# Where the projection of q and the state sums stand in TensorE's order, in a retention layer with a mixture of experts

## The chip, the cores and the metric

The kernel runs on one core of a Trainium2 chip. The metric is the device time of one execution in microseconds (us); lower is better. In the tables and rows PE is the tensor engine (PEld its weight loads), DVE the vector engine, ACT the scalar engine, POOL GpSimd and SP the engine whose queue issues most of the DMAs.

## The reference

Everything is float32. The input x has 4 batches of 1024 tokens with 256 channels. The first half is a retention layer with 16 heads of 16 channels, the second an expert layer; both have a residual.

```python
def attn(x):                       # on the layer norm of x
    q, k, v = x @ W_q.T, x @ W_k.T, x @ W_v.T      # split into 16 heads of 16
    decay = where(i >= j, gamma[head] ** (i - j), 0)
    a = einsum('bihd,bjhd->bhij', q, k) * decay / sqrt(16)
    y = einsum('bhij,bjhd->bihd', a, v)
    yn = (y - y.mean over tokens and head channels) / sqrt(var + 1e-5)
    return (yn * gn_weight + gn_bias) @ W_o.T
x = x + attn(layernorm(x))
x = x + ffn(layernorm(x))          # shared gated layer + two of 8 experts per token
```

The decay lets the product be computed in chunks: inside a chunk through scores, and across chunks through a state (the decayed sum of k times v of all earlier tokens) that is carried forward.

## The kernel before

**Phases.** The first half of the time is the retention phase, 16 steps h = 0 to 15, each over 256 tokens (a "part"): batch b = h // 4 and place in the batch s = h % 4. Behind it comes the expert phase, a loop over batches, which the diff doesn't touch. In the profiled execution step h = 0 begins at about 20.5 us and step 15 ends at about 225 us.

**Arithmetic.** A float32 product is made of three matmuls with operands that are split in a high and a low part (`split_product`, L289 to L296). A projection of 256 tokens is therefore 12 matmuls of 256 columns, all with line L294 in the profile.

**One step on TensorE** (`step`, L430). TensorE works on two parts at once, the scores and state of part h and the projections of part h + 1. The order before is: `project_k(h+1)` into `c_bank`, `state_sums(h)` (64 small matmuls, L378, into `a_bank`), in steps with s = 0 and b > 0 `head_means` (L408), `project_q(h+1)` into `b_bank`, `from_state(h)` (64 small matmuls of q with the state, L393, 48 of them where s = 0), `k_by_tokens(h+1)` (4 transposes, L343), then what is left of the previous batch (in s = 0 `head_vars` L412, in s = 1 `output_bias` L418, in s = 2 and 3 two `output` products each, 24 matmuls L294), `from_scores(h)` (L402), `project_v(h+1)`, `transpose_x(h+2)` (L304) and `scores(h+1)` (L364).

**One step on VectorE** (`step`, L870), strictly in this order: `mask_scores(h)` (4 operations, L782), `add_state(h)` (it waits for `state_sums(h)`; L792 or L795, then L798, which gives `s_ready`, and where s < 3 two small L803 that carry the state), `decay_k(h+1)` (L771, gives `kT_ready`), `decay_q(h+1)` (L776, gives `qT_ready`), in s = 0 `gn_spread` (four tiny operations, the last gives what `head_vars` waits for), the layer norm of part h + 3 (L748 to L761, with one tiny power on POOL in the middle), in s = 2 and 3 two residual sums (L861), `low_y(h)` (L812), `y_sums(h)` (L817), `low_x(h+2)` (L766), in s = 1 with b > 0 `low_wo` (L853).

**Waits that matter here.**

```python
# from_state(h), first lines                     # add_state(h)
pe.wait_ge(s_ready, h + 1)                       dve.wait_ge(s_done, h + 1)
# k_by_tokens(h), first line                     # project_k(h), first line
pe.wait_ge(kT_ready, h + 1)                      pe.wait_ge(xlo_ready, h + 1)   # low_x
```

`project_q` waits for nothing of its own in a step (L333); its bank `b_bank` was read out by `low_x`, for which `project_k` has waited. ScalarE copies between these: `spread_k` (L606) after `kT_ready`, `copy_k`, `high_y`, `high_x`, `copy_v`, and up to step 10 one piece of the expert weights (L638), which POOL then turns into its low part (L1068, `low_ffn`). In the steps h = 1 POOL also makes sums of the expert biases (L1107).

The order of every queue is written out by hand; only semaphores tie the engines to each other.

Of the kernel before, what the change touches and what calls it, by code (L numbers as in the profile page):

```python
# [17 lines left out]
PARTS = NBATCH * NSUP  # L18
# [35 lines left out]
def moe_retention(nc, xa, xs, wattn, gnw, gnb, sw1, sw3, sw2, w1, w2, sb1, sb3, b1, sb2, b2, decay, masks, out):  # L54
# [3 lines left out]
    with ExitStack() as ctx:  # L58
# [229 lines left out]
        def _(pe):  # L288
# [19 lines left out]
            def project_v(h):  # L308
                if h == 0:
                    pe.wait_ge(wlo_ready, 3)  # L310
                else:
                    pe.wait_ge(s_ready, h)
                for t in range(TILES):
                    w = [(xhi[:, c, t * P:(t + 1) * P], xlo[:, c, t * P:(t + 1) * P]) for c in range(CB)]
                    mm = split_product(a_bank[:, t * D:(t + 1) * D], w, [(wqkv_split.hi[:, 2, c, :], wqkv_split.lo[:, 2, c, :]) for c in range(CB)])
                mm.then_inc(v_done, 1)

            def project_channels(bank, i, done):
                x = [(xhi[:, c, :], xlo[:, c, :]) for c in range(CB)]
                for g in range(GROUPS):  # L320
                    w = [(wqkv_split.hi[:, i, c, g * P:(g + 1) * P], wqkv_split.lo[:, i, c, g * P:(g + 1) * P]) for c in range(CB)]
                    mm = split_product(bank[:, g * SUPER:(g + 1) * SUPER], w, x)
                mm.then_inc(done, 1)

            def project_k(h):
                pe.wait_ge(xlo_ready, h + 1)
                if h == 0:
                    pe.wait_ge(wlo_ready, 1)
                else:
                    pe.wait_ge(kexp_copied, h)  # L330
                project_channels(c_bank, 1, k_done)

            def project_q(h):  # L333
                if h == 0:
                    pe.wait_ge(wlo_ready, 2)
                project_channels(b_bank, 0, q_done)

            def k_by_tokens(h):
                pe.wait_ge(kT_ready, h + 1)
                for t in range(TILES):  # L340
                    for g in range(GROUPS):
                        o = (t * GROUPS + g) * P
                        mm = nc.tensor.transpose(c_bank[:, o:o + P], kT[:, g, t * P:(t + 1) * P], ident)  # L343
                mm.then_inc(kt_done, 1)
# [23 lines left out]
            def state_sums(h):  # L368

                pe.wait_ge(kexp_copied, h + 1)  # L370
                pe.wait_ge(v_copied, h + 1)
                for c in range(CPS):
                    n = 2 - c % 2
                    for g in range(GROUPS):
                        o = (g * CPS + c) * 32
                        for p in range(PAIRS):
                            r = g * PAIRS + p
                            mm = nc.tensor.matmul(a_bank[32 * p:32 * p + 32, o:o + n * 32].rearrange("p (n e) -> p n e", n=n),  # L378
                                                  kexp[:, c, r, :], vexp[h % 2][:, c, r, :].unsqueeze(1).broadcast_to([P, n, 32]),
                                                  start=(c == 0 and g == 0), stop=True, skip_group_check=True)  # L380
                mm.then_inc(s_done, 1)

            def from_state(h):
                pe.wait_ge(s_ready, h + 1)
                if h:
                    pe.wait_ge(y_stats, h)
                first = 0 if h % NSUP else 1
                for c in range(first, CPS):
                    for g in range(GROUPS):
                        o = g * SUPER + c * CH  # L390
                        for p in range(PAIRS):
                            at = slice(32 * p, 32 * p + 32)
                            nc.tensor.matmul(y_bank[at, o:o + CH], state[h % 2][at, g, c, :], qT[h % 2][at, g, c * CH:(c + 1) * CH],  # L393
                                             start=(c == first and g == 0), stop=False, skip_group_check=True)

            def from_scores(h):
                pe.wait_ge(pm_ready, (h + 1) * PAIRS)
                for c in range(CPS):
                    for g in range(GROUPS):
                        o = g * SUPER + c * CH  # L400
                        for p in range(PAIRS):
                            mm = nc.tensor.matmul(y_bank[32 * p:32 * p + 32, o:o + CH], vexp[h % 2][:, c, g * PAIRS + p, :],  # L402
                                                  pm[p][:, c * GROUPS + g, :], start=False, stop=True, skip_group_check=True)
                mm.then_inc(y_done, 1)

            def head_means(b, bank):
                pe.wait_ge(gn_aggr, b + 1)
                nc.tensor.matmul(bank[:, 0:GROUPS], headmean, y_mv[:, :, 0], start=True, stop=True).then_inc(gn_mean, 1)  # L408

            def head_vars(b, bank):  # L410
                pe.wait_ge(gn_e, b + 1)
                nc.tensor.matmul(bank[:, 8:8 + GROUPS], headmean, y_e[:], start=True, stop=True).then_inc(gn_var, 1)  # L412

            def output_bias(b, bank):

                pe.wait_ge(bb_ready, b + 1)
                for c in range(CB):
                    mm = nc.tensor.matmul(bank[:, 0:D], y_bb[:, c, :], wo_raw[:, c, :], start=(c == 0), stop=(c == CB - 1))  # L418
                mm.then_inc(ob_done, 1)

            def output(b, j, bank):
                if j == 0:
                    pe.wait_ge(ylo_ready, (b + 1) * NSUP)
                    pe.wait_ge(wolo_ready, b + 1)
                for i in range(2):
                    w = [(yhi[b % 2][:, c, 2 * j + i, :], ylo[b % 2][:, c, 2 * j + i, :]) for c in range(CB)]
                    mm = split_product(bank[:, i * D:(i + 1) * D], w, [(wo_hi[:, c, :], wo_lo[:, c, :]) for c in range(CB)])
                mm.then_inc(o_done, 1)

            def step(h):  # L430
                b, s = h // NSUP, h % NSUP
                if h + 1 < PARTS:
                    project_k(h + 1)
                state_sums(h)
                if b and s == 0:
                    pe.wait_ge(pm_ready, h * PAIRS + 1)
                    head_means(b - 1, p_bank[0])
                if h + 1 < PARTS:
                    project_q(h + 1)
                from_state(h)  # L440
                if h + 1 < PARTS:
                    k_by_tokens(h + 1)
                else:
                    transpose_x2(0, 0)
                    transpose_x2(0, 1)
                if b and s == 0:
                    head_vars(b - 1, p_bank[0])
                if b and s == 1:
                    pe.wait_ge(pm_ready, h * PAIRS + 2)
                    output_bias(b - 1, p_bank[1])  # L450
                if b and s >= 2:
                    for j in range(2 * (s - 2), 2 * (s - 2) + 2):
                        pe.wait_ge(pm_ready, h * PAIRS + (j + 1))
                        output(b - 1, j, p_bank[j])
                if h + 1 == PARTS:
                    transpose_x2(0, 2)
                    transpose_x2(0, 3)
                from_scores(h)
                if h + 1 < PARTS:
                    project_v(h + 1)  # L460
                    if h + 2 < PARTS:
                        transpose_x(h + 2)
                    scores(h + 1)

            def transpose_x2(b, j):

                half, c = j // CB, j % CB
                if j == 0 and not (isinstance(b, int) and b == 0):
                    pe.wait_ge(gelu_ready, b * NE)
                if c == 0:  # L470
                    pe.wait_ge(xn2_ready, b * 2 + (half + 1))
                for t in range(4):
                    mm = nc.tensor.transpose(t2_bank[j][:, t * P:(t + 1) * P],  # L473
                                             xl[:, 4 * half + t, c * P:(c + 1) * P], ident)
                mm.then_inc(t2_done, 1)
# [78 lines left out]
            for h in range(PARTS):  # L554
                step(h)
# [633 lines left out]
```

## Time and profile before

| | us |
|---|---|
| median of 3 runs | 468.68 |
| lowest and highest run | 466.65, 469.02 |
| the profiled execution, its own time | 470.15 |
| its span, first to last instruction | 468.3 |
| PE busy (matmuls) | 447.9 |
| DVE busy | 294.4 |
| ACT busy | 217.1 |
| POOL busy | 101.4 |
| mean granted TensorE clock, share of full | 0.982 |

The profiled execution took 470.15 us, of which 468.3 us are its span; the rest lies around it. Busy time of matmuls counts overlapping pieces once and has modelled ends, so the starts of matmuls are the better clock: the start of one group to the start of the next is what a group costs.

### The profile page before, as it was taken

Reading aid. Unit: us, or ns where it says so; the run is one execution under the profiler, and the core shown is the slowest. Engines: PE = TensorE matmul, PEld = TensorE weight load, DVE = VectorE, ACT = ScalarE, POOL = GpSimd, SP = SyncE. Lnnn points to the kernel's source line nnn. Section 1 sums busy time; section 2 is a strip of 40 time slices with the busy share of each in tenths; the row PEclk is TensorE's granted clock in tenths of the full one; section 3 lists DMA queues with packets and bytes.
Section 4 is the critical chain, followed back from the end, with each engine's and each line's share of the span. In section 5 each row is a group of like instructions: output and inputs, shape, how many; then the busy total and the mean of one; then the engine's idle time right before and its main releaser. Section 6 shows DMA issues by size and latency. Waiting matters only on the chain.

```text
span 468.3 us, 14948 instructions
## 1 busy us (share of the span) xinstructions
PE 447.9 (96%) x6574; PEld 411.6 (88%) x6574; DVE 294.4 (63%) x655; ACT 217.1 (46%) x416; POOL 101.4 (22%) x79
## 2 busy tenths in 40 slices
PE   6899998999898999978999999999999999999997
PEld 4899997989888999968798999889998899988996
DVE  6578986877789778685574644566445564455321
ACT  3455555544665535441525534355343552445521
POOL 2017522712326201410180110301103011030000
PEclk9999998999999999996999999999999999999999
DMA  7511242201531040200514010500105001030011
GB/s 255 196 56 72 70 149 82 70 25 49 168 153 71 3 161 26 92 3 1 203 69 179 1 46 1 225 0 0 45 0 224 0 0 45 2 132 0 1 46 45
DMA packets 9271, 34.75 MB, mean 74 GB/s; under 512 B 1665, under 2 KB 1921, under 8 KB 7041
## 3 DMA queue, kind: packets, MB, share of 16 engines
q1 hardware_dynamic: 8784, 33.15, 19.5%
q8 instruction: 45, 0.74, 0.7%
q10 hardware_dynamic: 432, 0.79, 0.6%
q14 instruction: 10, 0.07, 0.0%
HBM read 25.54 MB, written 8.39 MB: 72 GB/s over the span
## 4 chain that ended last, share of the span: by engine, by line
PE 84%; DVE 10%; issue 2%; ACT 1%; DMA 1%; POOL 0%; SPq 0%; DVEq 0%; ACTq 0%
PE bank L294 65%; PE bank L364 5%; PE bank L402 3%; DVE pm L782 3%; PE bank L393 3%; PE bank L378 2%; PE bank L473 2%; PE bank L343 2%; DVE wo_lo L853 1%; DMA xin<-xa 1%; PE bank L304 1%; DVE state L803 1%; PE bank L418 1%; ACT xhi L583 1%; DVE ln_st L917 1%
## 5 line engine op out<-in xcount | busy, mean ns | idle before, releaser
L688 ACT ACTIVATE xres<-bank,r1b 128x256 f32<-128x256 f32 x64 | 26.8, 469 | 55.5 <-PE bank L294 55.5
L673 ACT ACTIVATE sil<-bank,s1b 128x512 f32<-128x512 f32 x32 | 22.1, 689 | 63.0 <-PE bank L294 63.0
L294 PE MATMUL bank<-x2hi,sw_hi 128*128 128x512 f32 x128 | 51.0, 398 | 0.0
L294 PE MATMUL bank<-x2hi,sw_lo 128*128 128x512 f32 x128 | 50.9, 398 | 0.0
L294 PE MATMUL bank<-x2lo,sw_hi 128*128 128x512 f32 x128 | 50.3, 393 | 0.0
L949 DVE SCALAR_TENSOR_TENSOR gf<-bank,s3b,sil 128x512 f32<-128x512 f32 x32 | 23.9, 748 | 39.4 <-PE bank L294 39.4
L606 ACT ACTIVATE keo<-kT,msk 128x512 f32<-128x512 f32 x32 | 21.4, 715 | 56.2 <-DVE kT L771 56.2
L782 DVE TENSOR_TENSOR pm<-bank,msk 128x512 f32<-128x512 f32 x64 | 39.7, 681 | 6.2 <-PE bank L364 6.2
L294 PE MATMUL bank<-xhi,wqkv_hi 128*128 128x256 f32 x128 | 39.8, 311 | 2.3 <-DVE xlo L766 2.3
L967 DVE TENSOR_TENSOR xr<-bank,xr 128x256 f32<-128x256 f32 x32 | 13.6, 424 | 41.8 <-PE bank L294 41.8
L294 PE MATMUL bank<-xhi,wqkv_lo 128*128 128x256 f32 x128 | 36.4, 284 | 0.0
L294 PE MATMUL bank<-xlo,wqkv_hi 128*128 128x256 f32 x128 | 36.3, 284 | 0.0
L961 DVE TENSOR_TENSOR elo<-xres,ehi 128x512 fp32r<-128x512 f32 x32 | 22.1, 691 | 22.5 <-ACT ehi L692 22.5
L294 PE MATMUL bank<-x2lo,w_hi 128*128 128x256 f32 x128 | 36.2, 283 | 0.0
L294 PE MATMUL bank<-x2hi,w_lo 128*128 128x256 f32 x128 | 36.2, 283 | 0.0
L294 PE MATMUL bank<-x2hi,w_hi 128*128 128x256 f32 x128 | 36.2, 283 | 0.0
L1094 POOL TENSOR_TENSOR xr<-xr,slot_bias 128x2048 f32<-128x2048 f32 x4 | 18.5, 4626 | 81.7 <-DMA xr<-x_scratch 81.7
L294 PE MATMUL bank<-sw_hi,ghi 128*128 128x256 f32 x128 | 36.1, 282 | 0.0
L364 PE MATMUL bank<-qT,keo 32*128 32x64 f32 x1024 | 33.9, 282 | 2.3 <-DVE xres L861 2.3
L364 PEld LDWEIGHTS bank<-qT,keo 32*128 32x128 f32 x1024 | 31.7, 195 | 5.0 <-issue 5.0
L294 PE MATMUL bank<-w_hi,elo 128*128 128x256 f32 x128 | 36.0, 282 | 0.0
L294 PE MATMUL bank<-w_lo,ehi 128*128 128x256 f32 x128 | 36.0, 281 | 0.0
(119 smaller groups left out, 1277.8 us busy)
## 6 DMA issues: line engine op xcount, KB each, us to landing
xin<-xa SPq DMA_DIRECT2D x16, 256.0 KB, 3.8
w_raw<-w SPq DMA_DIRECT2D x8, 512.0 KB, 4.7
xres<-xs SPq DMA_DIRECT2D x4, 1024.0 KB, 5.0
x_scratch<-xres SPq DMA_DIRECT2D x4, 1024.0 KB, 4.9
xl<-x_scratch SPq DMA_DIRECT2D x4, 1024.0 KB, 5.6
xr<-x_scratch SPq DMA_DIRECT2D x4, 1024.0 KB, 4.8
out<-xr SPq DMA_DIRECT2D x8, 512.0 KB, 2.6
sw_raw<-sw SPq DMA_DIRECT2D x3, 512.0 KB, 4.9
```

Of the source, the lines that this page charges most:

```text
L294: mm = nc.tensor.matmul(o, w[c][l], x[c][r], start=first and c == 0 and j == 0, stop=last and c == n - 1 and j == 2)
L364: mm = nc.tensor.matmul(p_bank[p][:, o:o + CH], keo[at, c, g, :, :], qT[h % 2][at, g, c * CH:(c + 1) * CH], start=True, stop=True)
L393: nc.tensor.matmul(y_bank[at, o:o + CH], state[h % 2][at, g, c, :], qT[h % 2][at, g, c * CH:(c + 1) * CH], start=(c == first and g == 0), ...
L402: mm = nc.tensor.matmul(y_bank[32 * p:32 * p + 32, o:o + CH], vexp[h % 2][:, c, g * PAIRS + p, :], pm[p][:, c * GROUPS + g, :], start=Fals ...
L606: cp = nc.scalar.activation(keo[:, :, :, odd, :], kT[:].rearrange("p g (c j) -> p c g j", c=CPS), ACT.Copy, scale=parity[:, odd:odd + 1])
L673: nc.scalar.activation(sil[i % 2][:], h1_bank[i % 2][:], ACT.Silu, bias=s1b[:, m:m + 1]).then_inc(sil_ready, 1)
L688: ge = nc.scalar.activation(hf[q % 2][:, m, :], e_bank[q % 4][:, m * 2 * P:(m + 1) * 2 * P], ACT.Gelu, bias=r1b[:, e, m:m + 1])
L782: nc.vector.tensor_tensor(pm[p][:], p_bank[p][:].rearrange("p (a i) -> p a i", i=CH), causal.unsqueeze(1).broadcast_to([P, CPS * GROUPS, C ...
L949: nc.vector.scalar_tensor_tensor(gf[i % 3][:], h3_bank[i % 2][:], s3b[:, m:m + 1], sil[i % 2][:], ALU.add, ALU.mult).then_inc(gf_ready, 1)
L961: nc.vector.tensor_tensor(elo[k][:], hf[q % 2][:], ehi[k][:].bitcast(F32), ALU.subtract).then_inc(elo_ready, 1)
L967: nc.vector.tensor_tensor(xr[:, s, :], o_bank[s % 2][:, 0:D], xr[:, s, :], ALU.add).then_inc(o_ready, 1)
L1094: nc.gpsimd.tensor_tensor(xr[:], xr[:], slot_bias[:], ALU.add).then_inc(biased, 1)
```

## The change

`project_q(h+1)` is moved up in TensorE's order, from behind `state_sums(h)` (and `head_means`) to directly behind `project_k(h+1)`. `state_sums(h)` is then directly ahead of `from_state(h)`, but for `head_means` where there is one. It concerns the 15 steps with h + 1 < 16. No instruction is added or removed, and no other queue is touched.

```diff
                 if h + 1 < PARTS:
                     project_k(h + 1)
+                    project_q(h + 1)
                 state_sums(h)
                 if b and s == 0:
                     pe.wait_ge(pm_ready, h * PAIRS + 1)
                     head_means(b - 1, p_bank[0])
-                if h + 1 < PARTS:
-                    project_q(h + 1)
                 from_state(h)
                 if h + 1 < PARTS:
                     k_by_tokens(h + 1)
```

## Rows read from the trace of the kernel before

**Rows 1.** The page: busy time by engine, and the chain that ended last.

```profile
PE 447.9 (96%) x6574; PEld 411.6 (88%) x6574; DVE 294.4 (63%) x655; ACT 217.1 (46%) x416; POOL 101.4 (22%) x79
...
PE 84%; DVE 10%; issue 2%; ACT 1%; DMA 1%; POOL 0%; SPq 0%; DVEq 0%; ACTq 0%
```

**Rows 2.** Waits: engine, operation <- releaser; total us, times, longest us.

```profile
PE bank L393 <- DVE state L798: 4.5, 4, 1.7
```

**Rows 3.** Timeline, PE, step h = 2: start us, us, engine, line, operation.

```profile
43.17 0.39 PE L294 MATMUL bank<-xhi,wqkv_hi 128*128 128x256 f32 x1
...
44.58 0.28 PE L294 MATMUL bank<-xlo,wqkv_hi 128*128 128x256 f32 x1
44.79 0.91 PE L378 MATMUL bank<-vexp,kexp 128*32 128x64 f32 x64
45.62 0.39 PE L294 MATMUL bank<-xhi,wqkv_hi 128*128 128x256 f32 x1
...
47.25 1.10 PE L393 MATMUL bank<-qT,state 32*32 32x64 f32 x64
```

**Rows 4.** Timeline, PE: 24 large matmuls in a row, first start, next group's start.

```profile
97.18 0.36 PE L294 MATMUL bank<-wo_hi,yhi 128*128 128x256 f32 x1
...
100.23 0.49 PE L402 MATMUL bank<-pm,vexp 128*32 128x64 f32 x20
```

**Rows 5.** Timeline, DVE, step h = 2.

```profile
45.77 0.29 DVE L795 TENSOR_TENSOR state<-bank,state 128x128 f32<-128x128 f32 x1
...
46.42 0.39 DVE L803 TENSOR_SCALAR state<-state,msk 128x32 f32<-128x32 f32 x2
46.74 0.68 DVE L771 TENSOR_TENSOR kT<-bank,dec 128x512 f32<-128x512 f32 x1
...
52.69 0.69 DVE L766 TENSOR_TENSOR xlo<-bank,xhi 128x512 fp32r<-128x512 f32 x1
```

**Rows 6.** Timeline, step h = 9: the end of the state sums and what follows.

```profile
134.12 0.55 PE L378 MATMUL bank<-vexp,kexp 128*32 128x64 f32 x30 [0.44 <-issue]
...
134.73 0.29 DVE L795 TENSOR_TENSOR state<-bank,state 128x128 f32<-128x128 f32 x1 [0.69 <-PE bank L378]
```

**Rows 7.** Timeline, step h = 14: its start, the state's sum, the product that waits.

```profile
195.10 0.39 PE L294 MATMUL bank<-xhi,wqkv_hi 128*128 128x256 f32 x1
...
199.19 0.28 DVE L795 TENSOR_TENSOR state<-bank,state 128x128 f32<-128x128 f32 x1
...
199.85 0.36 PE L393 MATMUL bank<-qT,state 32*32 32x64 f32 x11 [0.60 <-DVE state L798]
```

**Rows 8.** Timeline, step h = 4 (s = 0): start, kT, head_vars, a gap.

```profile
64.62 0.39 PE L294 MATMUL bank<-xhi,wqkv_hi 128*128 128x256 f32 x1
...
68.72 0.68 DVE L771 TENSOR_TENSOR kT<-bank,dec 128x512 f32<-128x512 f32 x1
...
70.59 0.38 PE L412 MATMUL bank<-y_e,msk 128*128 128x2 f32 x2 [0.20 <-DVE y_e L833]
...
72.97 1.07 PE L402 MATMUL bank<-pm,vexp 128*32 128x64 f32 x28 [1.32 <-issue]
```

**Rows 9.** Timeline, PE, step h = 12 (s = 0): start and head_vars.

```profile
172.41 0.39 PE L294 MATMUL bank<-xhi,wqkv_hi 128*128 128x256 f32 x1
...
178.09 0.38 PE L412 MATMUL bank<-y_e,msk 128*128 128x2 f32 x2
```

**Rows 10.** Timeline, step h = 8: POOL's low part and DVE's carry.

```profile
121.45 2.39 POOL L1068 TENSOR_TENSOR w_lo<-w_raw,w_hi 128x1024 fp32r<-128x1024 f32 x1 [9.24 <-ACT w_hi L638]
...
122.15 1.86 DVE L803 TENSOR_SCALAR state<-state,msk 128x32 f32<-128x32 f32 x2
```

**Rows 11.** Timeline, POOL, step h = 2.

```profile
47.41 2.38 POOL L1068 TENSOR_TENSOR sw_lo<-sw_raw,sw_hi 128x1024 fp32r<-128x1024 f32 x1
```

**Rows 12.** Windows: stretch, length, busy time (instructions) of PE, PEld, DVE, ACT, POOL, PEclk, DMA share, GB/s.

```profile
64.60:78.90 14.30, 12.78 (x292) 11.61 (x288) 10.08 (x30) 6.44 (x14) 3.75 (x3) 0.88 0.41 132
...
143.80:158.80 15.00, 13.75 (x333) 12.76 (x326) 12.02 (x25) 7.64 (x15) 5.31 (x4) 1.00 0.13 48
...
209.30:220.00 10.70, 8.94 (x203) 8.54 (x204) 5.47 (x13) 0.79 (x3) 0.00 (x0) 0.52 0.02 4
```

## The prediction

> **What bounds the kernel now.** I read the page first. TensorE is busy for 96% of the span and is 84% of the chain that ended last, VectorE 10% [rows 1]. So a wait of TensorE in the retention phase is paid in full, unless TensorE is waiting there anyway. The list of waits says how often it stands at the product that is moved against the state sums: `from_state` waited for the state only 4 times, 4.5 us in all [rows 2], although there are 16 such products. The timeline of a plain step shows why. In step 2 `project_k` starts at 43.17, the state sums at 44.79, `project_q` at 45.62 and `from_state` at 47.25, without a gap [rows 3]. VectorE adds the state at 45.77, just behind the sums' modelled end of 44.79 + 0.91 = 45.70, and is through with it before 46.42 [rows 3, 5]. The 1.63 us of `project_q` cover this round trip through VectorE. The change takes the cover away.
>
> **The change in a plain step.** I count from the start of `project_k`.
>
> Before: `project_k` 1.62, sums 0.83, `project_q` 1.63, so `from_state` starts at +4.08 [rows 3].
>
> After, the two projections are one run of 24 large matmuls. Two runs of 12 would be 3.25 us, but 24 in a row take 100.23 - 97.18 = 3.05 [rows 4]: the first and the last matmul of a run, next to small ones, are 0.2 apart instead of 0.12, and one such pair goes. So the sums start at +3.05 and end, as modelled, 0.91 later at +3.96. Where VectorE was free and waiting, its first sum started 134.73 - (134.12 + 0.55) = 0.06 behind that end [rows 6]: +4.02. From the start of that sum to the first waiting product it was 199.85 - 199.19 = 0.66 [rows 7]: `from_state` starts at +4.68. The cost of a plain step is 4.68 - 4.08 = **0.60 us**.
>
> Two chains hang on it. The carry and `decay_k` follow the state: kT starts 46.74 - 45.77 = 0.97 behind the first sum and takes 0.68 [rows 5], so it is ready at about +5.67 and the transposes can start at about +5.72 (0.05 from such an end to the waiting matmul is an estimate from the 0.06 above). `from_state` ends at 4.68 + 1.02 = +5.70. That fits, with nothing to spare. And VectorE's whole round is 1.42 us later than before: kT started at 46.74 - 43.17 = +3.57, and will at +4.99. In step 2 `low_x`, for which the next `project_k` waits, ended at 52.69 + 0.69 - 43.17 = +10.21 [rows 5]. With 1.42 more that is +11.6, against a step of about 10.7 + 0.6 = 11.3 (step 3 began at 53.9). But step 2's layer norm was held up by POOL's operation [rows 11], by about half a microsecond as I read it, so +11.1 is nearer. VectorE just stays off the path. If not, h = 1 and 2, the shortest, cost up to 0.3 more each; the later steps are longer.
>
> Plain in this sense are h = 1, 2, 3, 5, 7, 11, 13: 7 x 0.60 = **4.20**.
>
> **Steps that pay nothing.** h = 6, 10 and 14 come behind `low_wo`, which makes VectorE late with the masks. In h = 14, the tightest, the first state sum starts at 199.19 - 195.10 = +4.09 for that reason alone [rows 7]. After the change the sums are done by +4.02. VectorE is still what comes last: **0**. The wait of `from_state` there is then simply the old one.
>
> **Steps with s = 0.** There `from_state` has 48 matmuls, 0.77 us instead of 1.02, so the transposes are held by kT.
> - h = 0: transposes at +5.72 after, 4.08 + 0.77 = +4.85 before: **0.85**.
> - h = 12: `head_vars` waits for four tiny operations behind `decay_q`. In h = 4, where it waited for them, it came 70.59 - 68.72 = 1.87 behind the start of kT [rows 8]. After the change that is 4.99 + 1.87 = +6.86. In h = 12 it stood at 178.09 - 172.41 = +5.68 [rows 9]: **1.18**.
> - h = 4: it stood at 70.59 - 64.62 = +5.97, so it comes 0.89 later. But soon behind it TensorE stood for 1.32 us with nothing to wait for that the profile shows ("issue") [rows 8], in a step whose DMA share is 0.41, against 0.13 in h = 10 [rows 12]. If its instructions came late behind that traffic, they come at the same distance from the step's start as before, and the gap shrinks by what TensorE is later. Ends: 0 and 0.89; I take the middle, **0.4**.
> - h = 8: here the carry took 1.86 us instead of 0.39 and ended at 124.01, 0.17 behind the end of POOL's operation at 123.84 [rows 5, 10]. kT therefore can't be much later than it was: the carry moves by 1.42, from 122.15 to about 123.6, and ends at about the same time. Ends 0 and 0.2, **0.05**.
> - h = 9 (s = 1) has the same collision, and a 0.44 us gap of the "issue" kind in its state sums [rows 6], which now come 1.43 us later in the step. Ends 0 and 0.3, **0**.
>
> **A new collision.** In h = 2 POOL's low part starts at 47.41, nearly a microsecond behind the carry at 46.42 [rows 5, 11]. POOL got there through a chain that begins with VectorE's layer norm of step 1. That norm starts 0.85 later (h = 0) plus 1.0 (in h = 1, where kT was already a little late), so POOL's operation moves to about 49.27. The carry moves by 0.85 + 0.60 and the 1.40 within the step, to about 49.27 as well. If POOL is first, the carry ends where POOL does, as in h = 8: 49.27 + 2.38 + 0.17 = 51.8 against 49.66, about 2.2 us more. Ends 0 and 2.2; the two are equal to the last digit, and I take half, **1.1**.
>
> The row says that the carry ended with POOL's operation. The Trainium skill has the rule for it (SBUF — State Buffer, "SBUF: two separate sides"): VectorE in its two-port mode and GpSimd lock a shared pair of ports for a whole instruction. By that rule the sum would hold either 0 or 2.2, never half, that is 475.3 or 477.5.
>
> **The sum.** 4.20 + 0.85 + 1.18 + 0.4 + 0.05 + 0 + 1.1 = 7.8 us. Step 15 has no projections and is unchanged, and the expert phase starts later by the same amount. The profiled execution took 470.15, so it would take 477.9; it lies 1.5 above the median. On the median the forecast is 468.68 + 7.8 = **476.4 us**.
>
> The terms' own ends give 4.20 + 0.85 + 1.18 = 6.2 and, with 0.6 for VectorE in h = 1 and 2, 10.4. `low_wo` meets POOL's residual bias in h = 5, 9 and 13 and may come out a half microsecond better or worse in each, which I estimate at 1.5 either way in all. That gives 473.4 to 480.6.
>
> **The rivals.**
> - *More half clock, 0.14.* In h = 4, with its 1.32 us gap, the mean granted clock was 0.88 over 14.3 us. Between the two levels, 2.4 and 1.2 GHz, that is 0.24 x 14.3 = 3.4 us at the lower, of which half is lost: 1.7. From 209 to 220 us it was 0.52, nearly all at 1.2 GHz [rows 12]. Waits of 0.6 us in nearly every step did not exist before. If two to four of them or of the denser ones in h = 4 and 12 bring the clock down, the time is 480 to 483. Against it: h = 10 had 15.00 - 13.75 = 1.25 us without a matmul in one wait, and its clock stayed at 1.00 [rows 12]. The Trainium skill speaks for this rival (TensorE: Matmul & The Clock Gate, "A second HAM failure mode: psum-queue depth-cycling"): frequent short idle spells between groups of matmuls make the clock fall and rise again.
> - *Less half clock: not slower, 0.11.* The 10.7 us at a clock of 0.52 cost some 5 us and the stretch in h = 4 costs 1.7 [rows 12]. The later arrival shifts both against whatever decides on the clock. If the gap in h = 4 shrinks and that stretch goes, and of the long one a third or more, 3.4 or more of the 7.8 us come back, which gives 470 to 473. It decides from 5.5 us on, when the time is within 0.5% of before.
> - *The run of 24 saves nothing, or VectorE becomes the bound, 0.12.* With no saving each of the ten paying steps costs 0.2 more: 478.4. The same comes out if `low_x` is 0.2 late in each.
> - *The round trip is hidden, 0.05.* The weights of `from_state` might be loaded while the state is added. But their loads read the state, and in the rows that wait the loads came with the matmuls [rows 7]. Then 469 to 470.
> - *The forecast itself, 0.58*, 474 to 479.
>
> **Numbers.** What a measurement of this kernel can tell from no change is about 0.5%, 2.3 us, so "slower" begins at 471.0. The forecast, the more-clock and the run-of-24 cases are slower (0.84); the less-clock case is split (0.05 slower, 0.05 same, 0.01 faster), the hidden case is 0.04 same and 0.01 faster. That is slower 0.89, same 0.09, faster 0.02. For 8 in 10 the range must take the forecast's, most of the 24 case and a part of both clock cases: **472 to 480.5**.
>
> **What would show it.** In the profile after, `from_state` should wait for the state in nearly every step, about 0.6 us of silence (0.7 by the weight loads) in plain ones, and the old waits in h = 6, 10 and 14 should stay as they were. The two projections should be one run with 3.05 us to the state sums. VectorE should have a new wait for L378 of about 1.5 us in each plain step. In h = 12 `head_vars` should wait for `gn_spread`. Wrong would be: a plain step longer than 11.4 us with waits at `project_k` (VectorE is the bound), a carry of more than 2 us in h = 2, a gap in h = 4 that keeps its 1.32 us, and more or fewer stretches at half clock than before.

## The result, and the profile after

The changed kernel takes 478.73 us (median of 4 runs, 477.37 to 480.23) against 468.47 for the kernel before: the ratio is 1.0233, 95% interval 1.0200 to 1.0266, or 10.3 us slower. The forecast was 476.4, with a range of 472 to 480.5.

The page of the changed kernel (first the busy time by engine, then the chain that ended last) answers to [rows 1]:

```profile
span 477.0 us, 14948 instructions
...
PE 445.4 (93%) x6574; PEld 409.9 (86%) x6574; DVE 293.5 (62%) x655; ACT 216.7 (45%) x416; POOL 101.2 (21%) x79
...
PE 84%; DVE 11%; issue 2%; DMA 1%; ACT 1%; POOL 0%; SPq 0%; DVEq 0%; ACTq 0%
```

The instructions are the same and so, nearly, is the busy time. TensorE's busy share fell from 96 to 93%: what grew is silence. The list of TensorE's waits says where (total us, times, longest us):

```profile
PE bank L393 <- DVE state L797: 14.0, 16, 1.7
...
PE bank L343 <- DVE kT L770: 1.8, 2, 1.7
PE bank L412 <- DVE y_e L832: 1.4, 3, 0.5
```

`from_state` waited for the state 4 times before, 4.5 us in all [rows 2]; now it waits in all 16 steps, 14.0 us in all. The other two waits are the chain behind it, for kT and for what `head_vars` needs.

Step 2 on TensorE, then on VectorE, in the order of time (line numbers behind the edit are one lower than before):

```profile
45.30 0.39 PE L294 MATMUL bank<-xhi,wqkv_hi 128*128 128x256 f32 x1
...
48.36 0.91 PE L378 MATMUL bank<-vexp,kexp 128*32 128x64 f32 x64
50.02 0.69 PE L393 MATMUL bank<-qT,state 32*32 32x64 f32 x34 [0.75 <-DVE state L797]
...
52.79 0.66 PE L343 MATMUL bank<-msk,kT 128*128 128x128 f32 x4 [1.67 <-DVE kT L770]
```

```profile
49.35 0.29 DVE L794 TENSOR_TENSOR state<-bank,state 128x128 f32<-128x128 f32 x1 [1.42 <-PE bank L378]
49.67 0.29 DVE L797 TENSOR_TENSOR state<-bank,state 128x128 f32<-128x128 f32 x1
50.00 2.14 DVE L802 TENSOR_SCALAR state<-state,msk 128x32 f32<-128x32 f32 x2
52.05 0.68 DVE L770 TENSOR_TENSOR kT<-bank,dec 128x512 f32<-128x512 f32 x1
```

Against [rows 3]: the sums start at 48.36 - 45.30 = +3.06, the product at +4.72 instead of +4.08, and VectorE now waits 1.42 us for the sums. Against [rows 5]: the carry takes 2.14 us instead of 0.39, and POOL's timeline has the reason beside it:

```profile
49.61 2.34 POOL L1067 TENSOR_TENSOR sw_lo<-sw_raw,sw_hi 128x1024 fp32r<-128x1024 f32 x1
```

It began at 49.61, before the carry at 50.00, and ended at 51.95; the carry was done at about 52.1, and kT, the transposes and the rest of the step behind it.

**Step by step.** A second profile of either kernel was taken (below). The lengths of the steps, from the start of one `project_k` to the next, are read off the timelines:

```
step                1     2     3     4     5     6     7     8     9    10    11    12    13
before          10.73 10.73 10.72 14.36 11.60 14.70 13.62 12.52 12.45 14.93 13.61 11.08 11.61
before, second  10.73 10.73 10.72 11.78 11.60 14.66 13.61 12.28 12.40 14.93 13.62 11.07 11.61
after           11.69 13.11 11.69 12.79 12.23 14.92 14.25 12.71 12.44 14.93 14.25 12.25 12.24
after, second   11.70 13.10 11.37 13.15 12.23 14.91 14.25 12.28 12.37 14.92 14.25 12.25 12.24
forecast, diff.  0.60  1.7   0.60  0.4   0.60  0     0.60  0.05  0     0     0.60  1.18  0.60
second pair     +0.97 +2.37 +0.65 +1.37 +0.63 +0.25 +0.64  0    -0.03 -0.01 +0.63 +1.18 +0.63
```

Step 0 is 0.91 and 0.95 longer (11.93 before; forecast 0.85), and step 14, up to the start of its scores, 14.92 against 14.28 (forecast 0). Here the second pair gives 0.90 and 0.65, which with its row above makes 10.8 us; the medians are 10.3 apart.

The two second profiles as a whole are 14.4 us apart (480.14 and 465.77), and not all of that lies in the table. TensorE starts step 0 at 22.55 instead of 20.47 us, 2.1 later, behind a stretch at half clock from 9 to 16 us that the other three profiles don't have; the scores of step 14 take 0.4 longer, and from the start of step 15 to the end it is 1.1 more. The last part is in the first pair too (1.0): a stretch at half clock, the lower of the two levels, begins in every profile near the end of step 14, and it ends about 2 us later within step 15 in the changed kernel. The first 9 us of step 15, before and after:

```profile
213.01:222.01 9.00, 7.32 (x160) 7.01 (x157) 6.27 (x15) 1.49 (x4) 0.00 (x0) 0.63 0.01 2
220.67:229.67 9.00, 7.33 (x151) 7.03 (x149) 6.00 (x14) 1.53 (x4) 0.00 (x0) 0.52 0.01 2
```

The granted clock was 0.63 in both profiles of the kernel before and 0.52 and 0.50 in those of the changed one. But it was 0.50 to 0.54 too in three of the kernels below (the change in three steps alone, the sums first, all together), and 0.62 in the changed kernel with the carry moved. So this 1.0 us is not shown to belong to the change.

### The profile page after: what moved, and what is told of

Its sections match the earlier page's. It is cut to its first block, busy times and chain, and to the rows that moved or that the text cites. A ratio compares the mean times of both kernels' runs of the same rounds, so it can differ in the third digit from the quotient of the medians.

```text
span 477.0 us, 14948 instructions
## 1 busy us (share of the span) xinstructions
PE 445.4 (93%) x6574; PEld 409.9 (86%) x6574; DVE 293.5 (62%) x655; ACT 216.7 (45%) x416; POOL 101.2 (21%) x79
## 4 chain that ended last, share of the span: by engine, by line
PE 84%; DVE 11%; issue 2%; DMA 1%; ACT 1%; POOL 0%; SPq 0%; DVEq 0%; ACTq 0%
PE bank L294 65%; PE bank L364 5%; PE bank L402 3%; PE bank L393 2%; PE bank L378 2%; DVE pm L781 2%; PE bank L472 2%; DVE wo_lo L852 1%; DMA xin<-xa 1%; PE bank L343 1%; PE bank L304 1%; DVE state L797 1%; DVE state L802 1%; DVE kT L770 1%; PE bank L418 1%
## 5 line engine op out<-in xcount | busy, mean ns | idle before, releaser
L294 PE MATMUL bank<-xhi,wqkv_hi 128*128 128x256 f32 x128 | 38.5, 301 | 2.7 <-DVE xlo L765 2.7
L294 PE MATMUL bank<-w_hi,ehi 128*128 128x256 f32 x128 | 35.9, 281 | 0.0
L294 PE MATMUL bank<-sw_lo,ghi 128*128 128x256 f32 x128 | 35.8, 280 | 0.0
```

What stands on the lines that cost most here:

```text
L294: mm = nc.tensor.matmul(o, w[c][l], x[c][r], start=first and c == 0 and j == 0, stop=last and c == n - 1 and j == 2)
```

## The experiments

**A second profile of the kernel before.** No edit.

> The kernel before, unchanged, for a second profile. Question: is the half-clock stretch in step h = 4, with the 1.32 us gap ahead of it, a property of the kernel or of that one execution? The profiled execution of before was 1.7 us above its median, as much as such a stretch costs. Theory A: the stretch is an accident of that execution. Then step 4 (start of project_k to start of the next) takes about 12.7 us instead of 14.36, the execution 468 to 469 us, and the steps without clock trouble keep their lengths to 0.05 us. Theory B: the stretch belongs to the kernel, step 4 takes 14.3 us again and the time is about 470.

It took 465.77 us, with a span of 463.8. The window over its step 4 (columns as in [rows 12]):

```profile
64.60:76.40 11.80, 11.44 (x292) 10.27 (x288) 9.92 (x30) 6.54 (x14) 3.75 (x3) 1.00 0.50 161
```

Step 4 is 11.78 long, at a clock of 1.00, and the 1.32 us gap is down to 0.17. All other steps up to 13 keep their lengths to 0.05, but for step 8 (0.24). Theory A holds, and more strongly than expected: the half clock and the length of the gap, 2.6 us in all, belong to the one execution on which the forecast rests. The gap itself belongs to the program. It stands behind 36 of the 64 matmuls L402 of step 4 in twelve of the thirteen profiles of this document, 0.17 to 1.32 us long; the two of the kernel before have the longest and the shortest:

```profile
71.83 0.64 PE L402 MATMUL bank<-pm,vexp 128*32 128x64 f32 x28 [0.17 <-issue]
```

The first profile also has 1.6 us more in step 14, with a longer stretch at half clock. Together that is why the first profiles of the two kernels are only 8.6 us apart (478.78 and 470.15) while the medians are 10.3 apart.

**A second profile of the changed kernel.** No edit.

> The changed kernel, unchanged, for a second profile. In the first, h = 1 and 3 were 0.91 and 0.97 longer than before and not 0.63 as h = 5, 7, 11 and 13, for a gap of about 0.3 us in the run of matmuls of each that nothing in the profile explains. If such gaps are accidents of an execution, as the 1.32 us of the kernel before was, h = 1 and 3 are now 11.36 each or have the gap elsewhere, while what the change itself does stays to 0.05 us: h = 2 at 13.1 (or 12.8 without a gap), h = 12 at 12.25, h = 14's product with the state 0.64 later than before. If they belong to the changed order, h = 1 and 3 are 11.69 again.

It took 480.14 us. Step 3 lost its gap (11.37), step 1 kept it: its 64 small matmuls L402 took 1.42 us in both profiles of the changed kernel and 1.10 in those of before.

```profile
41.76 1.42 PE L402 MATMUL bank<-pm,vexp 128*32 128x64 f32 x64
```

So the gap of step 3 is an accident, and that of step 1 came twice at the same place. Two profiles don't settle whether it belongs to the order; in the changed kernel with the carry moved (below), where TensorE's order is the same, these matmuls took 1.16 and step 1 was 11.43 long. Steps 2, 12 and 14 repeat: 13.10, 12.25, 0.64.

**The change in three steps alone.**

```diff
+                    if h in (6, 10, 14):
+                        project_q(h + 1)
                 state_sums(h)
...
-                if h + 1 < PARTS:
+                if h + 1 < PARTS and h not in (6, 10, 14):
                     project_q(h + 1)
```

> The change is made in h = 6, 10 and 14 alone, the steps behind low_wo, where VectorE is late with the masks. My theory: they pay nothing, the first state sum starts no later than before and the step lengths stay 14.70, 14.93 and 14.28 to 0.1 us; the time is that of before within 0.3 us. That h = 6 and 14 became 0.22 and 0.64 longer under the whole change then comes from VectorE's low_wo, which met POOL differently. Rival: these steps pay the 0.6 us too, then it is 0.9 to 1.9 us slower and the lengths show it here as well.

467.53 us; ratio 0.9987 (0.9964 to 1.0011). Steps 6 and 10 are 14.68 and 14.93 long. Step 14, its start, the first state sum and the product:

```profile
193.08 0.39 PE L294 MATMUL bank<-xhi,wqkv_hi 128*128 128x256 f32 x1
...
197.17 0.27 DVE L797 TENSOR_TENSOR state<-bank,state 128x128 f32<-128x128 f32 x1
...
197.83 0.87 PE L393 MATMUL bank<-qT,state 32*32 32x64 f32 x48 [0.78 <-DVE state L800]
```

The state sum starts at +4.09, exactly as in [rows 7], and the product at +4.75. The same edit that costs 0.63 us in a plain step costs nothing where VectorE is late anyway. What the full change added in steps 6 and 14 must come from elsewhere: under it VectorE's `low_wo`, just ahead of them, took 3.02 and 3.01 us instead of 2.79 and 2.37, and ahead of step 10, which did not move, 3.02 both times. The wait itself did not stay the old one, as forecast: it is 0.78 here for 0.60 in [rows 7], since the joined run of matmuls is over 0.19 sooner and the state is not.

**Half of the projection as cover.**

```diff
                     project_k(h + 1)
+                    project_channels(b_bank, 0, q_done, (0,))   # first 6 of 12 matmuls
                 state_sums(h)
...
-                    project_q(h + 1)
+                    project_channels(b_bank, 0, q_done, (1,))   # the other 6
                 from_state(h)
```

> Only the first 6 of the 12 matmuls of the projection of q go ahead of the state sums, the other 6 stay behind them. My theory (the cover): the product with the state waits because nothing stands between the sums and it while VectorE adds the state, about 0.73 us. Six matmuls are about 0.81 us of cover, so the wait is 0 to 0.1 us in plain steps, and a plain step is as long as before (10.73 in h = 2, 11.60 in h = 5). In h = 12 the four tiny operations come late and cost some 0.45, in h = 0 0.15. In all 0.5 to 1.5 us above before. Rival (it is the order of the two projections and the sums itself, a later s_done for VectorE's round, that costs): then half the delay costs half, some 0.3 us in each plain step and 4 to 5 us in all.

472.68 us; ratio 1.0101 (1.0070 to 1.0132), 4.8 us above before. By the total this is the rival's number. By the steps it isn't: 1, 3, 5, 7 and 13 are 10.74, 10.84, 11.60, 13.61 and 11.60 long, as before but for 0.12 in step 3, and step 12 is 11.52, the 0.45 that was forecast. Most of what is left sits in step 2, 14.71 long. Its waits:

```profile
PE bank L394 <- DVE state L800: 5.8, 4, 2.3
PE bank L344 <- DVE kT L773: 3.7, 3, 2.4
```

The state is waited for 4 times, as before; one wait for kT, of 2.4 us, stands in step 2, where the carry was held for 2.94 us. Behind it came 4 us at a clock of 0.57, which make up the rest of that step's 4.0:

```profile
51.50:55.50 4.00, 4.00 (x77) 3.67 (x76) 2.82 (x10) 3.20 (x7) 0.73 (x1) 0.57 0.00 0
```

Step 4 has a gap of 0.9 us, step 14 is 0.5 longer up to its scores (`low_wo` took 2.91 us ahead of it). The total spoke for the wrong theory, because the collision is sharp: the carry came 0.7 us later within the step than before, and its two operations met two of POOL's in a row, the last sum of the expert biases and then the low part.

**The carry behind the decays, in the changed kernel.** `carry_state` is the tail of `add_state` (the two L803) as a function of its own; the edit that cuts it out is left out here.

```diff
                 if b and s == 0:
                     gn_spread(b - 1, p_bank[0])
+                carry_state(h)
                 if h + 3 < PARTS:
                     ln_sums(h + 3)
```

> The changed kernel, and VectorE does the two small carry operations of the state behind decay_k, decay_q and gn_spread instead of ahead of them. My theory: of the change's 10 us, about 1.7 in h = 2 (carry held until POOL's operation ends, kT behind it) and 0.3 to 0.5 in each step with s = 0 (kT and head_vars hang on VectorE's chain) go away, some 3 us: 475 to 476.5. The wait of the product with the state stays 0.75 us in plain steps. Rival: kT is not what TensorE waits for there, or the held carry blocks what comes behind it as long; then it is 478 to 479.

473.75 us; ratio 1.0124 (1.0081 to 1.0167) to before, 5 us under the changed kernel. Step 2 on VectorE: kT now stands ahead of the carry.

```profile
49.02 0.29 DVE L797 TENSOR_TENSOR state<-bank,state 128x128 f32<-128x128 f32 x1
49.22 0.68 DVE L770 TENSOR_TENSOR kT<-bank,dec 128x512 f32<-128x512 f32 x1
49.82 0.68 DVE L775 TENSOR_TENSOR qT<-bank,dec 128x512 f32<-128x512 f32 x1
50.42 1.22 DVE L806 TENSOR_SCALAR state<-state,msk 128x32 f32<-128x32 f32 x2
```

The carry is still held (1.22), but step 2 is 11.74 long instead of 13.11. The plain steps 5, 7, 11 and 13 stay at 12.23, 14.24, 14.25 and 12.24: their 0.63 has nothing to do with the carry. Steps 6, 8, 9, 10 and 12 gain 0.38, 0.59, 0.21, 0.37 and 0.14, and step 14 is 0.56 shorter up to its scores. More came back than the 3 us expected, since I had not seen that steps 6, 10 and 14 hang on VectorE as well.

**The same in the kernel with half the projection as cover.** Both edits above.

> Half of the projection of q as cover, and the carry behind decay_k, decay_q and gn_spread. The half projection alone was 4.8 us slower than before, but its plain steps were as long as before (10.74, 11.60, 13.62); 4.0 us of it stood in h = 2, where the transposes waited 2.4 us for kT behind a carry held by POOL. My theory: with kT ahead of the carry that wait is gone, h = 2 is 10.7 to 11.2 long, and the time is 466 to 468.5, that of before or a little less. Rival: half a projection ahead of the sums costs by itself; then the plain steps stay and yet 3 us or more above before remain.

467.18 us; ratio 0.9993 (0.9960 to 1.0026). With the wait for kT gone, no difference to the order with the whole cover can be told. Step 2 is 11.73 long, somewhat more than I allowed, since the carry, held for 1.93 us, now delays the layer norm behind it.

**The same in the kernel before, as a control.**

> The kernel before with the carry moved alone: the control for the two kernels that combine it with another order. In the changed kernel it gave 0.37 in h = 6 and 10, 0.6 in h = 8, 0.2 in h = 9. Expected here: the same four or five steps get shorter by 0.2 to 0.6 each and the plain ones stay at 10.73, 11.60, 13.61, together 1 to 2 us faster than before, 466 to 467. Rival: the carry costs only where the changed order has made VectorE late; then no difference.

467.03 us; ratio 0.9985 (0.9951 to 1.0020): no difference that can be told. In the steps the gain is there (6, 9 and 10 are 14.28, 12.01 and 14.28, that is 0.38, 0.39 and 0.65 less than in the second profile of before), but step 2 is 11.49 instead of 10.73 and step 12 11.37 instead of 11.07, and that takes most of it back. So of the 5 us that the carry gave the changed kernel the larger part was the change's own doing.

**Another cover.** On the changed kernel with the carry last: `decay_k` and `decay_q` ahead of `add_state` on VectorE, and

```diff
+                if h + 1 < PARTS:
+                    k_by_tokens(h + 1)
                 from_state(h)
-                if h + 1 < PARTS:
-                    k_by_tokens(h + 1)
...
```

> The changed order with another cover: VectorE does decay_k and decay_q ahead of the state, and TensorE the transposes of k between the state sums and the product with the state (the carry last, as above). My theory: the cover counts, not what it is. The 0.58 us of transposes then hide most of the 0.73: a wait of 0.15 to 0.3 at the product in plain steps, which are 0.1 us from before (10.6 to 10.8 in h = 1 and 3, 11.5 to 11.7 in h = 5). In h = 6, 10 and 14 the state comes 1.2 later behind the masks, half of it is paid, 0.6 each. In all 468 to 470. Rival: small matmuls next to small matmuls of another tile shape, or the missing run between them, cost by themselves; then the plain steps stay near 11.3 and the time near 474.

467.63 us; ratio 0.9992 (0.9964 to 1.0021). The state sums and the projections stand as in the changed kernel; only the 0.58 us of transposes now lie between the sums and the product. Step 2 of it:

```profile
44.38 0.39 PE L294 MATMUL bank<-xhi,wqkv_hi 128*128 128x256 f32 x1
...
47.45 0.91 PE L378 MATMUL bank<-vexp,kexp 128*32 128x64 f32 x64
48.28 0.66 PE L343 MATMUL bank<-msk,kT 128*128 128x128 f32 x4
...
49.10 1.10 PE L393 MATMUL bank<-qT,state 32*32 32x64 f32 x64 [0.16 <-DVE state L797]
```

The product still starts at 49.10 - 44.38 = +4.72, when the state is there, but the transposes have been done by then and the wait is 0.16 instead of 0.75. The step is 10.79 long, as expected. It is the only plain step of which that is true: steps 1, 3, 5, 7, 11 and 13 are 11.48, 11.17, 11.85, 13.83, 13.84 and 12.04, that is 0.22 to 0.75 longer than before. Step 1 has a gap without a releaser, and in step 3 the product waits 0.47. In 5, 7 and 11 the wait is 0.16 as in step 2, and about 0.2 more is lost behind the product, where the transposes no longer stand between small matmuls and large ones. In step 5 the large `output_bias` (L418) now has small matmuls on both sides and takes 1.06 to the next group instead of 0.96, and the transposes have lost the place ahead of it where they took 0.49; the two rows are from this kernel:

```profile
83.96 1.13 PE L418 MATMUL bank<-wo_raw,y_bb 128*128 128x256 f32 x4
85.02 1.10 PE L402 MATMUL bank<-pm,vexp 128*32 128x64 f32 x64
```

So the rival, that the order of the groups costs by itself, is right to about 0.2 us in these steps and doesn't explain the 0.63: the wait went with the cover put back. By the medians this edit gave 6.1 us and the carry 5.0, and both together bring the time back to that of before. A part of the 6.1 comes from the steps in which VectorE's decays now stand ahead of the state (step 8 is 11.74 long and `head_vars` is waited for nowhere in the phase).

**The sums first.** Both projections in one run, as in the change, but behind the state sums; the carry last; ScalarE copies v ahead of x.

```diff
+                state_sums(h)
                 if h + 1 < PARTS:
                     project_k(h + 1)
-                state_sums(h)
+                    project_q(h + 1)
...
-                if h + 1 < PARTS:
-                    project_q(h + 1)
                 from_state(h)
```

> The state sums go to the head of the step, directly behind the scores, and both projections in one run behind them (carry late, and ScalarE copies v ahead of x so that the sums needn't wait for v). It keeps what the change gains, one run of 24 matmuls instead of two of 12, and has the whole run as cover. My theory: no wait at the product with the state in plain steps, which are 0.19 us shorter than before (10.54, 11.41, 13.42), some 2 us in 12 steps, and with the carry's gain 463.5 to 466. Rivals: the sums wait for the copy of v, or the later copy of x makes low_x and with it the projection of k late; then the plain steps are 10.7 to 11.2 and the time is 466 to 471.

468.77 us; ratio 1.0049 (1.0012 to 1.0085), 0.5% slower, where 463.5 to 466 was expected: a miss. In steps 1 and 2 it does what was expected, 10.53 and 10.54 us:

```profile
42.56 0.91 PE L378 MATMUL bank<-vexp,kexp 128*32 128x64 f32 x64
43.40 0.39 PE L294 MATMUL bank<-xhi,wqkv_hi 128*128 128x256 f32 x1
...
46.45 0.76 PE L393 MATMUL bank<-qT,state 32*32 32x64 f32 x40
```

That shows the 0.19 us of the single run; 7 and 11 are 13.44 and 13.42. But in the steps where VectorE is late with the masks the product is no later for it and waits, in step 6 for 3.4 us:

```profile
89.06 3.85 DVE L856 SCALAR_TENSOR_TENSOR wo_lo<-wo_raw,y_a,wo_hi 128x256 fp32r<-128x256 f32 x2
92.83 2.47 DVE L781 TENSOR_TENSOR pm<-bank,msk 128x512 f32<-128x512 f32 x4
...
95.88 1.39 PE L393 MATMUL bank<-qT,state 32*32 32x64 f32 x44 [3.40 <-DVE state L797]
```

Neither of my rivals was the reason there: `low_wo` took 3.85 us, since it met POOL's residual bias and then its low part. The granted clock fell during those 3.4 us and was 0.51 from 94.5 to 101.5, and step 6 is 19.30 long. A gap of 1.8 us without a releaser came on top in step 9. But this profiled execution took 473.53 us; it is one of four of the ten with 471.6 or more, and the other six took 467.8 to 468.9. How much of the loss at the median comes from step 6 is not shown.

**low_wo ahead of the layer norm.** On the kernel before with the carry last.

```diff
                 carry_state(h)
+                if b and s == 1:
+                    low_wo(b - 1)
                 if h + 3 < PARTS:
                     ln_sums(h + 3)
```

> The kernel before with the carry last, and low_wo (VectorE, 1.5 us by itself, 2.4 to 3.0 where POOL holds it up) ahead of the layer norm in steps h = 5, 9 and 13 and not at their end. Theory: it takes place in VectorE's slack and away from POOL's residual bias, so that the masks of h = 6, 10 and 14 are in time and the product with the state there waits 0 to 0.3 instead of 0.6 to 1.2; low_x comes up to 0.7 late in h = 5, 9 and 13. Net 0.3 to 0.7 in each of three steps, 1 to 2 us under the kernel with the carry last: 465 to 466. Rival: what low_wo saves behind it loses ahead of it; then 467.

467.68 us; ratio 0.9998 (0.9975 to 1.0022), no gain. `low_wo` takes 0.88 us here, so that its work by itself is 0.9 us and not the 1.5 of my expectation. Steps 6 and 10 are 13.61 each, 0.67 less than with the carry last alone, and step 14 is 1.00 shorter up to its scores, but 5 and 9 are 12.59 and 12.75, 0.99 and 0.74 more. POOL's residual bias now meets the layer norm instead (0.74 us before):

```profile
83.25 0.88 DVE L857 SCALAR_TENSOR_TENSOR wo_lo<-wo_raw,y_a,wo_hi 128x256 fp32r<-128x256 f32 x2
...
86.12 5.07 POOL L1068 TENSOR_TENSOR xres<-xres,o_bias 128x512 f32<-128x512 f32 x4
86.19 2.65 DVE L761 TENSOR_SCALAR xin<-xin,ln_mv,ln_r 128x256 f32<-128x256 f32 x2 [0.81 <-POOL ln_r L1051]
```

**All together.** The last kernel, with the sums first in `SUMS_FIRST = (1, 2, 5, 7, 11, 13)` and, for these, v copied ahead of x.

```diff
+                first = h in SUMS_FIRST
+                if first:
+                    state_sums(h)
                 if h + 1 < PARTS:
                     project_k(h + 1)
-                state_sums(h)
+                if first:
+                    project_q(h + 1)
+                else:
+                    state_sums(h)
...
-                if h + 1 < PARTS:
+                if h + 1 < PARTS and not first:
                     project_q(h + 1)
```

> The version to beat both: the last kernel, and in h = 1, 2, 5, 7, 11 and 13, where VectorE is in time with the masks, the state sums at the head of the step and both projections in one run behind them (with v copied ahead of x for those steps). With the sums first in every step these were 10.53 long instead of 10.73, but where VectorE was late the product waited up to 3.4 us. Theory: 0.2 us in each of six steps, 1.2 in all, on top of the last kernel: 463.5 to 465.5, 0.5 to 0.9% under before. Rival: the later copy of x costs it again; then 465 to 467.

466.80 us; ratio 0.9966 (0.9931 to 1.0002), where 463.5 to 465.5 was expected: a miss. Steps 1, 7 and 11 are 10.54, 13.42 and 13.41 long, the 0.2 us expected. Steps 2, 5 and 13, at 11.53, 12.89 and 11.57, are not: in the last kernel they were 11.49, 12.59 and 11.61. The whole is 0.3% faster at the median, and the interval takes in 1: not shown to beat the kernel before.

## Why the prediction was right, and which terms were off

**Right, and shown.** The mechanism: `project_q` was the cover of VectorE's round trip between the sums and the product. Three kernels that put a cover back have a plain step of 10.74 us (half the projection, step 1), 10.79 (the transposes, step 2) and 10.54 (the run of 24 itself, step 2) against 10.73 before and 11.37 after (step 3, second profile). The cleanest is half the projection, with six plain steps within 0.12 us of before; the transposes leave a wait of 0.16 and cost some 0.2 more in other steps. The plain step was forecast at 0.60 us and measures 0.63, with all its parts: sums at +3.06 (forecast +3.05), product at +4.72 (+4.68). The saving of the single run, 0.19, shows in the kernel with the sums first. Step 12 was forecast at 1.18 and is 1.18: `head_vars` came at 185.47 - 178.62 = +6.85, forecast +6.86. That steps 6, 10 and 14 pay nothing by themselves is shown by the kernel with the change in these alone. VectorE stayed off the path in the plain steps.

**The collision in step 2** was mis-sized. I took 1.1, half of a whole or nothing; it was the whole, and with 2.14 us for the carry one of my own signs of being wrong came. The difference of step 2 is 2.37, of which 0.63 is the plain cost and 1.74 the collision (forecast ends 0 and 2.2). A term that is either 0 or 2 should not stand at half in a forecast that names the likeliest time. The row of step 8 [rows 10] had shown that the carry ends with POOL's operation. By the rule of the Trainium skill (SBUF — State Buffer, "SBUF: two separate sides") whoever comes first holds the shared ports for its whole instruction, and with both at the same time that excludes the half. The traces agree: in steps 1, 5, 8 and 9 of the kernel before and 2 of the changed one the carry met POOL's low part, and each time it ended 0.2 to 0.4 us behind it. In the changed kernel POOL was 0.39 us ahead (49.61 against 50.00). My working had put the two at the same time, so that it was the whole was not foreseen. Step 1 had come out 0.37 longer than forecast, which is most of the lead; but the carry was held in step 2 of the kernel with half the projection too, whose step 1 has its old length. There the carry took 2.94 us, in the changed kernel with the carry moved 1.22.

**Step 4** was mis-sized, 0.4 against 1.0 to 1.4 (from 11.78). I let TensorE's delay shrink a gap of 1.32 us whose length was an accident of one execution. `head_vars` came at 76.96 - 70.10 = +6.86, just as worked out. Without the gap the step is 11.78 - 0.17 = 11.61 long before and 12.79 - 0.30 = 12.49 after, which is 0.88, the upper end, 0.89. The kernel with the change in three steps alone, which has the old order in step 4, gives the same 12.46 - 0.86 = 11.60, and the second profile of the changed kernel the same 13.15 - 0.66 = 12.49. The rest, 0.1 to 0.5, is the length of the gap, which changes between profiles. That it is late instructions was only argued and was not tried.

**Steps 6 and 14** were set at 0 and cost 0.25 and 0.64. I had named the place, `low_wo` against POOL's residual bias, but given it only to the range and not to the sum. The growth of `low_wo` matches both in size (0.23 and 0.64), and its meeting with POOL sets it. In the three steps of either kernel it ends 0.28 or 0.29 us behind POOL's residual bias, as in step 13 before and after:

```profile
191.41 5.19 POOL L1063 TENSOR_TENSOR xres<-xres,o_bias 128x512 f32<-128x512 f32 x4 [7.05 <-ACT o_bias L630]
194.51 2.37 DVE L853 SCALAR_TENSOR_TENSOR wo_lo<-wo_raw,y_a,wo_hi 128x256 fp32r<-128x256 f32 x2
...
200.05 5.18 POOL L1062 TENSOR_TENSOR xres<-xres,o_bias 128x512 f32<-128x512 f32 x4 [8.32 <-ACT o_bias L629]
202.51 3.01 DVE L852 SCALAR_TENSOR_TENSOR wo_lo<-wo_raw,y_a,wo_hi 128x256 fp32r<-128x256 f32 x2
```

Where it was moved ahead of the residual bias it took 0.88 us.

**Step 1** is 0.97 instead of 0.60: its matmuls L402 took 0.32 longer in both profiles. The cause is open.

**The clock rivals** did not come in steps 1 to 13. Step 4 lost its stretch at half clock, as the rival on the other side had it, but so did the kernel before in its second profile, so it was no effect of the change. Waits of 0.75 us in nearly every step left the granted clock at its upper level, 2.4 GHz, as the window from step 0 into step 14 of the changed kernel shows (1.00 behind the busy times):

```profile
26.00:210.00 184.00, 166.93 (x4349) 153.40 (x4338) 138.50 (x334) 96.86 (x194) 61.11 (x52) 1.00 0.24 79
```

In two other orders it did fall, at one long wait: with half the projection as cover just behind 2.4 us without a matmul, with the sums first within 3.4. The Trainium skill's page TensorE: Matmul & The Clock Gate ("A second HAM failure mode: psum-queue depth-cycling") tells of a kernel in which frequent short idle spells brought the clock down. The waits of 0.75 us did not do so here. What the rivals did not name is step 15, which I had called unchanged: from its start on both profiles of the changed kernel are 1.0 to 1.1 us longer, for a clock of 0.52 and 0.50 instead of 0.63 in its first 9 us. The rival that VectorE becomes the bound and the one that the round trip is hidden are out with the lengths of the plain steps.

So the sum was 7.8, and the second pair of profiles gives 10.8 up to the scores of step 14: the difference is 0.7 from the collision, about 0.9 from steps 6 and 14, 1.0 from step 4, 0.4 from step 1, 0.1 from step 0, and the rest from 0.03 to 0.05 in the other plain steps. By the medians it is 10.3. The terms that were off by more than 0.05 all erred to the same side, and the time stayed within the range, whose upper end was 480.5, with 1.8 us to spare. How near the table comes to the medians is in part luck, since step 4 alone changes by 2.6 us between two profiles of one kernel.

## What to carry to other kernels

Where one engine's result goes through another engine and back, ask what stands between the two: here half a projection, 0.8 us, was enough, the transposes left a wait of 0.16, and without any cover 0.63 us were lost per step, though nothing was added and even 0.19 saved. Ask then what else hangs on the engine that the round trip goes through, since a delay of 0.7 to 1.4 us there moved one small operation behind another engine's long one and cost as much as three plain steps. And profile the kernel before more than once: an accident in the only profile was worth 2.6 us, a quarter of the effect, and the second profile had the shortest such gap of all.

## What the runs showed of the hardware that was not expected

A pair of small VectorE operations, 0.39 us by itself, took 2.14 us when POOL's operation of 2.34 us had begun 0.39 us earlier, and 0.78 when POOL's of 2.39 us had begun 1.80 earlier (step 1 before): what it loses is what is left of POOL's. Moving the victim let the next one be hit: the carry (2.14), `low_wo` (2.4 to 3.9 for 0.9 us of work), the layer norm (2.65 for 0.74). TensorE's stream had gaps of 0.2 to 1.8 us without a releaser. The one in step 4 stood behind the same matmul in twelve of thirteen profiles and its length changed, from 0.17 to 1.32 in two executions of one program, while nine of the other steps repeat to 0.01 us. A run of 12 large matmuls between small ones costs 1.62 us, of 24 3.06: joining two runs saves 0.19.
